# Layer 0's items: the context rows are requested by the sync engine, and results are transposed in one pass

## The reference

```python
x = x + tanh(g_xattn[0]) * L0_xattn(layernorm(x), ctx, kv_mask, q_mask, ...)   # 16 heads of 64, softmax over 1500 keys
x = x + tanh(g_ffn[0])   * L0_ffn(layernorm(x), ...)                           # 16 experts, top 4, shared expert
x = x + tanh(g_xattn[1]) * L1_xattn(layernorm(x), ctx, ...)                    # slot attention, 3 iterations with a GRU
x = x + tanh(g_ffn[1])   * L1_ffn(layernorm(x), ...)                           # 32 experts, top 2, capacity 68
```

```python
dots = einsum('bhid,bhjd->bhij', q, k) * scale
attn = softmax(where(q_mask & kv_mask, dots, mask_value))
out = einsum('bhij,bhjd->bhid', attn, v)          # then out @ Wout + bout
```

## Time and profile before

| | |
|---|---|
| median of 3 runs | 579.34 us (575.66 to 580.33) |
| the profiled execution | 580.25 us, span in the profile 578.4 us |
| items, from the first scores to the last transposed result | 86.8 to 154.4 us |
| busy over the span | PE 77%, DVE 58%, ACT 54%, POOL 45% |
| DMA over the span | 74.10 MB, mean 128 GB/s |

### The profile page before, as it was taken

How to read it: one execution, slowest core, us unless ns; L and a number is a source line. 1 busy time by engine, 2 the same in 40 slices (tenths; PEclk the granted TensorE clock), 3 DMA queues, 4 the chain that set the end, 5 groups by cost and what they waited for, 6 DMA issues and landing times.

```text
span 578.4 us, 17285 instructions
## 1 busy us (share of the span) xinstructions
PE 443.8 (77%) x6312; PEld 335.0 (58%) x6312; DVE 334.4 (58%) x916; ACT 315.0 (54%) x905; POOL 260.3 (45%) x476
## 2 busy tenths in 40 slices
PE   2893988889679999669999988899998574059910
PEld 1631324556554454458888878888898443049910
DVE  0669964677734655357777766777777326014512
ACT  1573673555412222099999988899999221025400
POOL 9294762223420000236776777766776500700044
PEclk9696996999896999689999999999999855569965
DMA  8862644444149911500000299300000397130112
GB/s 308 304 227 87 218 160 123 135 135 135 54 130 344 342 46 37 255 2 3 3 2 0 82 344 326 118 3 2 0 0 2 124 425 324 55 87 22 40 50 69
DMA packets 47346, 74.10 MB, mean 128 GB/s; under 512 B 4428, under 2 KB 40828, under 8 KB 46140
## 3 DMA queue, kind: packets, MB, share of 16 engines
q1 hardware_dynamic: 42796, 60.51, 31.5%
q0 software_dynamic: 1472, 8.72, 4.2%
q10 hardware_dynamic: 3024, 4.13, 2.3%
HBM read 69.75 MB, written 3.60 MB: 127 GB/s over the span
## 4 chain that ended last, share of the span: by engine, by line
PE 55%; DVE 18%; POOL 9%; issue 7%; ACT 5%; DMA 3%; ACTq 1%; POOLq 1%; DVEq 1%; SPq 0%
PE ps L1582 12%; PE ps L1566 8%; PE ps L1500 5%; PE ps L1408 4%; DVE ps L1207 4%; PE ps L1696 3%; PE ps L1708 3%; PE ps L1516 2%; DVE sm L1218 2%; POOL work L712 2%; POOL xe_scratch L753 2%; PE ps L1380 2%; POOL early_w L758 2%; PE ps L1480 2%; PE ps L1590 1%
## 5 line engine op out<-in xcount | busy, mean ns | idle before, releaser
L867 ACT ACTIVATE work<-ps,nb,rkey 125x56 f32<-125x56 f32 x576 | 173.5, 447 | 5.5 <-DVE nb L1211 5.5
L1566 PE MATMUL ps<-work,region 128*61 128x56 f32 (+1 forms) x2304 | 77.8, 224 | 6.9 <-ACT work L867 5.0
L1566 PEld LDWEIGHTS ps<-work,region 128*61 128x61 f32 (+1 forms) x2304 | 75.6, 140 | 7.5 <-issue 7.4
L1582 PE MATMUL ps<-region,work 125*64 125x129 f32 x1152 | 71.5, 279 | 6.4 <-POOL work L712 3.1
L1582 PEld LDWEIGHTS ps<-region,work 125*64 125x64 f32 x1152 | 65.1, 139 | 11.8 <-POOL work L712 9.3
L712 POOL TENSOR_TENSOR work<-work,rs 125x336 f32<-125x336 f32 x96 | 69.9, 749 | 3.8
L1207 DVE TENSOR_REDUCE ps<-ps 125x12 f32<-125x672 f32 x48 | 41.6, 866 | 36.9 <-PE ps L1566 36.8
L1218 DVE TENSOR_REDUCE sm<-work 125x12 f32<-125x672 f32 x48 | 40.6, 845 | 5.1 <-ACT work L867 4.6
L1408 PE MATMUL ps<-xln,folded 128*128 128x448 f32 x64 | 29.9, 592 | 10.2 <-ACT region L793 10.2
L758 POOL DMA_INDIRECT early_w<-ys_scratch,gidx x14 | 13.3, 950 | 52.1 <-DMA ys_scratch<-folded 48.1
L778 ACT ACTIVATE region<-early_w 125x1536 f32<-125x1536 f32 x16 | 23.7, 1490 | 17.1 <-DVE sumsq L987 12.9
(11 more groups left out here) (290 smaller groups left out, 972.6 us busy)
## 6 DMA issues: line engine op xcount, KB each, us to landing
early_w<-in_ctx SPq DMA_DIRECT2D x16, 768.0 KB, 4.8
region<-in_ctx SPq DMA_DIRECT2D x16, 768.0 KB, 9.4
region<-in_w SPq DMA_DIRECT2D x6, 2048.0 KB, 18.7
region<-in_ctxT SPq DMA_DIRECT2D x16, 750.0 KB, 11.0
work<-in_ctxT_blk SPq DMA_DIRECT2D x22, 187.5 KB
early_w<-in_w POOLq DMA_DIRECT2D x1, 4096.0 KB, 12.3
region<-in_ctx_blk ACTq DMA_DIRECT2D x11, 192.0 KB, 2.8
early_w<-in_ctx_blk ACTq DMA_DIRECT2D x10, 192.0 KB, 2.4
```

Of the source, the lines that this page charges most:

```text
L867: i = act.activation(shares_of(u, a)[:, h, c, :], ps[:CP, 2 + 2 * a + h, c * S:(c + 1) * S], ACT.Exp, bias=nb[:, a, q:q + 1], scale=rkey[: ...
L1566: mm = pe.matmul(ps[r0:r1, 2 + 2 * a + h, c * S:(c + 1) * S], keysT[:, s, q * CP + r0:q * CP + r1], qT[:, p, a * S:(a + 1) * S], start=Tru ...
L1582: mm = pe.matmul(ps[i * COL:(i + 1) * COL, 6, 0:KW], A[:CP, u, i, h, c * S:c * S + COL], keys[:CP, 2 * p + i, h * CH + c, :], start=(h == ...
```

## The change

Two edits.

First, the requests for the context rows go from ACT to SP. `load_rows(j, k)` now stands in SP's loop behind `load_item(j + 2, k)`, reads the block number of item j for itself, and waits for `o_mm >= j + 1`, the product of item j-2, which used the same buffer. On ACT the request for item j+1 stood behind the copy of `PT` for j, which had waited for the product of j-1. SP's two first `load_item` calls move ahead of its loop, and its last wait goes. The last, unused, row request of before is no longer made (20 instead of 21).

Second, the transpose of the result is written as `pe.transpose` instead of a product with the identity.

```diff
@@ sync engine
+            def load_rows(j, k):
+
+                blk = sp.value_load(item_blk[0:1, bass.ds(j, 1)], min_val=0, max_val=B * KB - 1)
+                sp.wait_ge(o_mm, j + 1)
+                sp.dma_start(ictx[k], t["ctx_blk"][bass.ds(blk, 1), :, :].rearrange("a p (c d) -> (a p) c d", c=KC)).then_inc(ld_item[k], 16)
+
+            for k in range(AHEAD):
+                load_item(k, k)
             with sp.Fori(0, (n + 1) // 2) as i:
                 for k in range(2):
-                    load_item(sp.snap(i * 2 + k), k)
-            for k in range(AHEAD):
-                load_item(sp.snap((n + 1) // 2 * 2 + k), k)
-            sp.wait_ge(ld_item[0], (n + 1) // 2 * 16 + 16)
+                    load_item(sp.snap(i * 2 + (k + AHEAD)), k)
+                    load_rows(sp.snap(i * 2 + k), k)
@@ scalar engine
-            def load_rows(j, k):
-
-                blk = act.value_load(item_blk[0:1, bass.ds(j, 1)], min_val=0, max_val=B * KB - 1)
-                act.dma_start(ictx[k], t["ctx_blk"][bass.ds(blk, 1), :, :].rearrange("a p (c d) -> (a p) c d", c=KC)).then_inc(ld_item[k], 16)
-
             act.wait_ge(items_ok, 1)
             n = act.value_load(item_n[0:1, 0:1], min_val=1, max_val=ITEMS)
-            load_rows(0, 0)
...
                     act.copy(PT[:KP].rearrange("p c r -> p (c r)"), ps[:KP, 2, 0:KC * 128]).then_inc(pt_ev, 1)
-                    load_rows(j + 1, 1 - k)
                     probabilities(j + AHEAD, k)
@@ tensor engine
-                pe.matmul(ps[:, 4, 0:128], On, ident[:, :], start=True, stop=True).then_inc(ot_mm, 1)
+                pe.transpose(ps[:, 4, 0:128], On, ident[:, :]).then_inc(ot_mm, 1)
```

## The result

| | before | changed |
|---|---|---|
| median | 578.36 us (18 runs, 575.66 to 581.51) | 585.9 us (18 runs, 578.26 to 588.09) |
| ratio | 1 | **1.009**, 95% interval 1.006 to 1.012 |
| profiled execution | 580.25 us, span 578.4 | 586.99 us, span 585.2 |
| pace of the items (requests of `ictxT`, items 5 to 21) | 2.82 us | **3.29 us** |
| first product of the output projection | 155.86 us | 162.05 us |

The runs of the changed kernel scatter over 10 us. The medians, over all runs, differ by 7.5 us or 1.3%.

What follows compares the result with a forecast made beforehand. The chain of waits bounded the kernel before; SP would bound the changed one. Row requests +13.7, early +0.3, late -1.0, last transpose -0.3 sum to +12.7 us, on 579.34 giving 592 us, range 584 to 599.

Steps and rivals of the forecast that it cites:

- What bounds the kernel: Items' stage: a chain of waits through PE, DVE and ACT sets 2.82 us an item; SP has 0.75 us of room.
- the price of `load_rows`: SP's loop: requesting the rows costs 1.55 us an item against 0.75 of room, 13.7 us in all.
- The second way of counting: SP's whole turn without waits: 3.73 us against 2.82, so 0.91 too much an item, 14.6 us over 16 items.
- the lower bound: Rows' request on SP at ACT's price plus 0.1 us: 1.15 instead of 1.55 us, 6.4 us less in all.
- The ends of the stage: First and last items: +0.3 us at the start, -1.0 at the end, -0.3 for the last transposed result.
- Early: Start of the items' stage: `ictxT` requests shift from 99.07 to 99.4 by item 5, +0.3 us.
- Late: End of the items' stage: last request to end of last scores takes 4.6 instead of 5.6 us, -1.0; last transpose -0.3.
- The wait on `o_mm`: SP ahead of the next `load_item`: the product ends about 5.8 us after the request, SP arrives at 9.4; costs nothing.
- Rival 1: SP's loop: the rows' request fits in SP's 0.75 us of room and rows come in time; 577.7 us, chance 0.12.
- Rival 2: Items' stage: PE's clock falls to half and PE becomes the bound; 597 us, up to 611, chance 0.10.
- The signs: Changed profile: requests 3.6 to 3.8 us apart, no SP waits, POOL awaiting masks, PE near 0.6, stage end near 167.

Runs made afterwards that it cites:

- the transpose alone: Kernel before with only the second edit, the result transposed in one pass, row requests left on ACT: 578.61 us, ratio 1.001.
- e6: Changed kernel with one more, unused, read of the list in each load_item on SP: 596.2 us, ratio 1.030.
- e4: Changed kernel with the mask row's request moved from SP to ACT, behind the copy of PT: 600.16 us, ratio 1.035.
- e3: Changed kernel with the rows' request always taking block 0, without reading the list: 577.13 us, ratio 0.999.
- e5: Changed kernel with SP reading the list once per item, the block number held in a register for the rows: 579.07 us, ratio 1.001.
- e9: Changed kernel with one list read per item on SP, and ACT keeping the result ahead of the exponentials: 577.12 us, ratio 0.999.
- e12: Kernel before with one more, unused, read of the list in each load_item on SP: 578.51 us, ratio 1.001.

## Why the prediction was wrong in size

I forecast +12.7 us and 592, with a range from 584 to 599. The measured ratio means +5.2 us, the medians differ by 7.5, and the spans of the two profiles by 6.8. The direction and the mechanism were right, the cost was about twice too high.

**What bounds the kernel.** Right: SP had 0.75 us of room in an item, and it was filled. The run with an extra read in the kernel before confirms the room directly, and the runs with one read less in the changed kernel that this room is what was overrun.

**The step that failed is the price of `load_rows`: "1.20 + 0.345 = 1.55 us", and the 13.7 us made from it.** The pace rose by 3.288 - 2.822 = 0.466, over 16 items 7.5 us, not 13.7. Two things were mis-sized, both in the 1.20 us that I put between two requests:

- I took it from one instance "with hardly a wait", the one at 90.37 in the earlier trace rows, and distrusted it rightly. Behind the mask's request the gap is 115.27 + 0.28 = 115.55 to 116.63, 1.08 us. So 0.12 of it had been waiting: the scores it waits for ended at 90.14 (L1438, 89.65 + 0.49), and the next register instruction of L528 starts at 90.2. The second way of counting held the sign of it, since 2.03, 0.15 for the branch and the 0.75 of waits make 2.93 for a turn that took 2.82.
- I used it for both gaps of the new turn. Behind the rows' request it is 116.63 + 0.35 = 116.98 to 117.88, 0.90 us. The list's read there takes 0.27 and not 0.43: the first read after a mask request is the slow one, and the change brings a second read that is not. The kernel before had the sign of it. Its reads behind a mask request took 0.43 to 0.45, and its very first one, at 72.7 with no mask request ahead of it, took 0.294.

Together 0.42 us a turn too much, 6.7 us over 16 items, about the miss of this term (6.2). The price over SP's old turn is 3.288 - (2.822 - 0.75) = 1.22 us, close to the 1.15 that ACT's rows gave. I had that as the lower bound, "If SP paid that and 0.1 us more", and 586 as its result; the median came to 585.9. I set it aside because SP's reads take 0.43, and read a property of the place as one of the engine. That 1.15 comes so near is partly luck: the new request itself holds a slow read and takes 1.08 + 0.35 = 1.43 us, and what makes up for it is that `load_item`'s own read, now second, has become the fast one. A whole read, with its bounds check and register work, cost 0.57 and 0.66 us in the two runs that added one. The Trainium skill's floor of 600 ns for a register load ("DMA: Bandwidth & Descriptors", Latency and other measured facts) is met by neither single load, 0.27 or 0.43 us.

**The ends of the stage.** Early: forecast +0.3, measured 98.14 against 99.07, -0.9; from the request for item 2 to that for item 5 the transpose alone was 1.2 us shorter than before as well, so part of this may be scatter. Late: forecast -1.0 and -0.3. From the last request to the end of the last scores it is 4.6 us (150.75 to 155.37) instead of 5.6, as forecast. But from there to the output projection it is 6.7 instead of 6.0: PE waits 0.76 us instead of 0.31 for DVE's result of the item before, and the clock falls to half at about 158.8 us, ahead of the last transposed result, and not behind it as before (155.8). That result took 0.48 us in one pass at the half clock, against 0.49 in two at the full one, so the 0.3 us forecast for it, which was high even at the full clock (0.33 against 0.49), did not appear against the kernel before. Late in all: -0.3 instead of -1.3. The two misses of about 1 us cancel, which is luck. Sum by the profile: 7.5 - 0.9 - 0.3 = 6.2, and the output projection starts 6.2 us later. The span is 6.8 us longer, so 0.6 us more are lost behind it; the stretch at half clock is 6.8 us long there where it was 3.4.

**The wait on `o_mm`** cost nothing, as worked out: no wait of SP for a product is in the items' stage of the changed profile.

**Rival 1, hidden:** fell, though the rest of what it says holds: with the load out of SP's turn the time is that of before, and the gain I gave it (1.6 us) is too small to see. **Rival 2, the clock:** fell in the form that I gave it. With PE at 0.75 of the stage the clock stayed full from 98 to 156 us. The Trainium skill's sentence that a transpose-mode pass doesn't count as activity ("TensorE: Matmul & The Clock Gate", Part 4: PE-mode transpose) is neither borne out nor refuted by that. At the thinner pace of 3.86 (e6, PE busy 28.77 of 42 us, 0.69) one stretch at half clock does stand in the middle of the stage, from about 133 to 137 us, where the changed kernel had none.

**The signs** named ahead: even requests and no waits on SP, right, but 3.1 to 3.5 us apart and not 3.6 to 3.8; POOL waiting for the mask in 19 items, right; PE's share 0.75 and not 0.6; the stage's end, the last transposed result, at 160 and not 167.

## What to carry to other kernels

An engine that only issues transfers has a turn like any other: add up its register loads, waits and issues, and hold its waiting time in the trace against what is moved to it; 0.75 us of room do not take a request of 1.2. Price each instruction in the place where it will stand, since the same register load cost 0.27 or 0.43 us with different requests ahead of it, and prefer two measured bounds to one instance that may hide a wait. A request that is moved must be asked both ways: what is queued behind it on the new engine, and whether the work ahead of it there now belongs to the ring of those who wait for its data, as with the mask on ACT.

## What the runs showed of the hardware

- A register load from SBUF on SP took 0.43 us when it was the first one after the request of the mask row (375 bytes in one partition), and 0.27 us otherwise: 0.430 and 0.273 in the changed kernel, 0.269, 0.268 and 0.438 for the three reads of e6, 0.27 for all in e4, where SP requests no mask. In e3, e5 and e9, where the rows' request stands between the mask's and the read, it is still 0.43. Why, no run shows.
- A whole read (load, bounds check, register work) cost 0.57 us of SP's time in e6 and 0.66 in e12, more than the issue of a 192 KB transfer, 0.34.
- With SP as the bound the others stand idle for part of each item: from 90 to 160 us of the changed kernel POOL waited 46.7 us for the mask, ACT 35.1 for the maximum, DVE 19.4 and PE 12.6. SP has no busy time in the first part of a profile's page, so that part doesn't show the bound; the chain does.
